# The order of the causal row maxima in a decoder layer's attention: query tiles 2, 3, 0, 1, two heads at a time

## The chip, the core and the metric

One core of one Trainium2 chip runs the whole kernel. The metric is the device time in microseconds (us) of one execution. The engines are TensorE (PE, with its weight loads as PEld), VectorE (DVE), ScalarE (ACT), GpSimd (POOL) and SyncE (SP, which issues most of the DMAs).

## The reference

A decoder layer on x of 8 batches x 512 tokens x 256 features, 16 attention heads of 16 features each:

```
x = x + selfattention(layernorm(x))          # rotary positions, no mask
x = x + (causal selfattention + crossattention with ctx)(layernorm(x)) @ Wp
x = x + moe(x)                               # 16 experts, top 1, capacity 256

att = einsum(q, k) * scale
att = where(tril(ones(T, T)), att, -inf)     # the causal part
y   = einsum(softmax(att), v)
```

So each batch has three attentions: A (without mask), B (causal) and C (with the context). The softmax takes the maximum of each query's row of scores off before the exponential; in B the row of a query ends at its own position.

## The kernel before, in words

**Bodies and slots.** The work is a chain of bodies, numbered -2 to 24 (`plan`, line 257). Bodies 0 to 7 do the A attention of the eight batches; from 8 to 23 a B body (even) and a C body (odd) alternate, one batch for each pair. Bodies 10 to 21 are a hardware loop of six rounds. In bodies 11, 13, ..., 21 (and 23, 24) a batch is also routed to its experts. The experts themselves run at the end, after body 24. Each body has 32 slots. In each slot, every engine's program goes through the same list: it does its share of the maxima, of the exponents, of the product with V, and of the jobs that stand at this slot in a table written by hand (`SLOTS_OF`, line 61; the causal bodies use the entry `BB`, the C bodies `CC`, body 7 `AB`).

**Maxima.** A body has 64 units: 8 pairs of heads x 4 query tiles of 128 x 2 heads of a pair. A slot does two units, the two heads of one pair at one query tile, and it runs 12 slots ahead (`LEAD`, `s_unit` line 446): a body's first 12 slots of maxima run in slots 20 to 31 of the body before, and slots 0 to 19 of the body itself do the rest. `pair_of` (line 452) gives unit u its pair of heads, u // 8, and its query tile, u % 8 // 2. In `maxima` (line 747) TensorE makes the scores of 128 queries against the keys, n columns (line 764): 512 in A and C, and (query tile + 1) x 128 in B, where four masking products (lines 772 and 776) follow. VectorE reduces each half to the negated maximum of its rows (line 1193), into a column of `negmax`. The scores stand in a ring of three buffers, two for each slot: before a slot's scores TensorE waits until the first half of the slot before has been reduced (`max_done`, line 759).

**Hand-over.** Sixteen units make a group of four heads. Two slots after its last unit (slots 5, 13, 21 and 29) TensorE transposes the group's maxima (line 867), ScalarE and VectorE write them as two half-precision rows (lines 1070 and 1296), and SyncE sends these by DMA (line 598) into the stack of queries, so that the product of line 795 takes the maximum off by itself. The exponents' products of a group's first slot (0, 8, 16, 24) wait for that DMA (line 789).

**Exponents.** In slot t TensorE makes the transposed scores of key tile t % 8 // 2 for two heads (line 795; in B 512, 512, 384, 384, 256, 256, 128 and 128 columns over eight slots, in A and C 512 always), and ScalarE their exponentials (line 1029). The product with V (line 741) follows three and four slots later; after each group ScalarE copies it out (line 1021).

**Other work of VectorE around the change.** In a causal body the layer norm of the batch two bodies ahead has its steps in slots 2, 5, 6 and 7 (`layernorm`, line 1137: statistics, small operations, GpSimd's power at line 1427, then the normalizing at line 1165); slot 8 transposes its result (line 831). In slot 7 follows the reciprocal of the softmax sums of the body before (line 1200), which goes to memory and back by DMA, to two products on GpSimd (lines 1473 and 1477) and to ScalarE's cast in slot 16 (line 1001). In the routing C bodies (from 11 on) VectorE makes the one-hot choice in slot 26 (lines 1340 to 1346), TensorE counts with it in slot 27 (line 888), and VectorE works out the places in slot 28 (lines 1350 to 1367). On VectorE the reduces stand first in each slot, then the reciprocal and the norm, then the hand-over, then the routing.

Of the kernel before, what the change touches and what calls it, by code (L numbers as in the profile page):

```python
# [34 lines left out]
P = 128  # L35
NB, T, D, DC = 8, 512, 256, 128
H, HD = 16, 16
TT = T // P
# [267 lines left out]
def need(eng, sem, value):  # L306

    if not isinstance(value, int) or value > 0:
        eng.wait_ge(sem, value)


def build(nc, a):
    blocks, total = plan()
    ctx = ExitStack()
    with ctx:
# [130 lines left out]
        def s_unit(b, t, j):  # L446

            u = 2 * (t + LEAD) + j
            later = u >= S_UNITS
            return later, u % S_UNITS, 2 * t + j if b.kind else 2 * t + j - 2 * (SLOTS - LEAD)  # L450

        def pair_of(u):

            return u // 8, u % 8 // 2

        def has_s(b, later):
            return b.nxt if later else b.kind
# [11 lines left out]
        def stack_of(parity, q_or_k):  # L469
            return stack[:, parity, q_or_k, :].rearrange("p (h t) -> p h t", h=PAIRS)  # L470
# [218 lines left out]
        def _(pe):  # L689
# [24 lines left out]
            for b in stretches(pe, blocks):  # L714
# [11 lines left out]
                for t in range(SLOTS):  # L726
# [20 lines left out]
                    def maxima():  # L747
                        later, u, k = s_unit(b, t, 0)
                        kind = has_s(b, later)
                        if not kind:  # L750
                            return
                        par = np_ if later else b.parity
                        hp, qt = pair_of(u)
                        if later and u == 0:
                            if b.n in (-1, 0):
                                pe.wait_ge(stack_set, 16 * 4)
                            pe.wait_ge(s["stack_in"], b.at("stack_in", 16 * len(LOADS)))

                        need(pe, s["max_done"], b.at("max_done", k - 1))
                        n = (qt + 1) * P if kind == "B" else T  # L760
                        banks = S_BANKS[u // 2]
                        for hh in range(2):
                            rows = slice(PART * hh, PART * hh + STACK)
                            mm = nc.tensor.matmul(psS[:, banks[hh], 0:n], stack_of(par, 0)[rows, hp, qt * P:(qt + 1) * P],  # L764
                                                  stack_of(par, 1)[rows, hp, 0:n], start=True, stop=kind != "B",
                                                  skip_group_check=kind == "B")
                            if kind != "B":
                                mm.then_inc(s["scores_q"], 1)
                        if kind == "B":
                            for hh in range(2):  # L770
                                rows = slice(PART * hh, PART * (hh + 1))
                                nc.tensor.matmul(psS[:, banks[hh], n - P:n], unit_a[rows, :], mask_q[rows, :], start=False,  # L772
                                                 stop=False, skip_group_check=True)
                            for hh in range(2):
                                rows = slice(PART * hh, PART * (hh + 1))
                                mm = nc.tensor.matmul(psS[:, banks[hh], n - PART:n], unit_b[rows, :], mask_q[rows, 0:PART],
                                                      start=False, stop=True, skip_group_check=True)
                                mm.then_inc(s["scores_q"], 1)


                    def exponents():
# [18 lines left out]
                        if b.kind == "B":  # L800
# [4 lines left out]
                            for hh in range(2):  # L805
# [3 lines left out]
                                mm.then_inc(s["scores_k"], 1)  # L809

                    maxima()
                    exponents()
                    if t in b.warm_job:
# [305 lines left out]
        def _(dve):  # L1119
# [50 lines left out]
            for b in stretches(dve, blocks):  # L1170
# [3 lines left out]
                for t in range(SLOTS):  # L1174
# [6 lines left out]
                    for j in range(2):  # L1181
                        later, u, k = s_unit(b, t, j)
                        kind = has_s(b, later)
                        if not kind:
                            continue
                        g = u // (S_UNITS // NG)
                        at = TT * (2 * j + u % 16 // 8) + u % 8 // 2
                        n = (u % 8 // 2 + 1) * P if kind == "B" else T
                        if u % (S_UNITS // NG) == 0:

                            need(dve, s["negmax_rows"], b.at("negmax_rows", t // 8 if b.kind else 0))
                        dve.wait_ge(s["scores_q"], b.at("scores_q", k + 1))
                        nc.vector.tensor_reduce(negmax[:, g % 2, at:at + 1], psS[:, S_BANKS[u // 2][j], 0:n], AX_X, ALU.max,  # L1193
                                                negate=True).then_inc(s["max_done"], 1)
# [407 lines left out]
```

## Time and profile before

| | |
|---|---|
| time of the runs shown | 1627.76, 1622.08, 1626.52 us; median 1626.52 |
| span of the profiled execution | 1626.3 us (its own time is not listed apart) |
| busy share of the span | PE 89%, PEld 40%, DVE 74%, ACT 65%, POOL 40% |
| reduces of line 1193 | 1536, 869.4 us busy |
| bodies | body 8 begins at 521.6 us, body 23 at 1337.9 us |

A row of the timeline has the start and the length of a group of like instructions, its engine, line, operation and tiles; in brackets, how long the engine had been idle before it, and what released it. A row of the windows has, for one stretch, the busy time of each engine and the number of its instructions, then TensorE's mean granted clock as a share of full speed, and the DMA engines' share and GB/s.

### The profile page before, as it was taken

To read this page: it belongs to the slowest core of one execution; us is meant where nothing else is said; L and a number is where in the kernel's file an instruction comes from. 1 tells how busy PE (TensorE), PEld (TensorE's weight loads), DVE (VectorE), ACT (ScalarE), POOL (GpSimd) and SP (SyncE) were. 2 spreads that over 40 slices of the span, in tenths; PEclk is the share of its full clock that TensorE was granted. 3 is DMA by queue.
4 is the path that set the end of the run, shared out by engine and by line. 5 is a ranking of instruction groups with operands and counts; after the bars stand their busy time and mean duration, and the time that the engine had idled before them with its cause. 6 is when DMAs were issued, how large, how long until landed. Compare 5 with 4: busy or idle time off the path is not lost.

```text
span 1626.3 us, 37857 instructions
## 1 busy us (share of the span) xinstructions
PE 1443.6 (89%) x14610; PEld 647.8 (40%) x14610; DVE 1204.3 (74%) x2434; ACT 1062.0 (65%) x2139; POOL 650.5 (40%) x535
## 2 busy tenths in 40 slices
PE   3799999999999898898998989989989978779997
PEld 1222322333333433334334244333343432359997
DVE  6788878888876776776877877768778677537774
ACT  2377777778777676676676676766766656425662
POOL 2544565466422422236145333352352211225554
PEclk8699999999999999999999999999999999889999
DMA  6435344444323433323323322332333211157771
GB/s 179 115 119 141 105 112 115 120 115 112 92 60 95 110 88 101 90 83 104 82 83 88 104 80 69 96 98 71 85 100 97 60 45 39 48 189 262 251 259 62
DMA packets 119479, 175.82 MB, mean 108 GB/s; under 512 B 26273, under 2 KB 85895, under 8 KB 114696
## 3 DMA queue, kind: packets, MB, share of 16 engines
q1 hardware_dynamic: 111376, 158.50, 34.4%
q0 software_dynamic: 5888, 14.24, 2.7%
q8 instruction: 108, 1.77, 0.5%
q10 hardware_dynamic: 2048, 0.83, 0.2%
q14 instruction: 59, 0.48, 0.1%
HBM read 102.33 MB, written 51.18 MB: 94 GB/s over the span
## 4 chain that ended last, share of the span: by engine, by line
PE 54%; DVE 17%; DMA 9%; ACT 6%; issue 6%; POOL 5%; SPq 2%; POOLq 0%; DVEq 0%; ACTq 0%
PE psO L741 13%; PE psM L466 9%; PE psS L764 9%; DVE negmax L1193 9%; PE psK L466 6%; PE psK L795 6%; PE psS L466 4%; ACT probs L1029 4%; DMA recipB<-recip_scratch 3%; PE psK L693 2%; DVE xn L1165 2%; DMA shared<-shared 1%; DVE stats L1141 1%; DMA stack<-mrows 1%; PE psM L831 1%
## 5 line engine op out<-in xcount | busy, mean ns | idle before, releaser
L1193 DVE TENSOR_REDUCE negmax<-psS 128x1 f32<-128x512 f32 (+3 forms) x1536 | 869.4, 615 | 273.6 <-PE psS L764 136.4
L1029 ACT ACTIVATE probs<-psK 128x512 f32<-128x512 f32 (+3 forms) x1536 | 753.7, 544 | 325.3 <-PE psK L795 198.4
L741 PE MATMUL psO<-probs,V 128*32 128x256 f32 (+1 forms) x5632 | 446.1, 389 | 23.8 <-ACT U L1021 17.8
L764 PE MATMUL psS<-stack 48*128 48x512 f16 (+3 forms) x1536 | 284.5, 367 | 57.2 <-DVE negmax L1193 53.7
L795 PE MATMUL psK<-stack 50*128 50x512 f16 (+3 forms) x1536 | 278.5, 359 | 26.1 <-DMA stack<-mrows 14.7
L764 PEld LDWEIGHTS psS<-stack 48*128 48x128 f16 x1536 | 74.2, 93 | 373.2 <-DVE negmax L1193 290.7
L741 PEld LDWEIGHTS psO<-probs,V 128*32 128x32 f32 x5632 | 113.5, 109 | 210.9 <-issue 122.8
L1427 POOL TENSOR_TENSOR rstd<-lnt,minus_half 128x4 f32<-128x4 f32 x24 | 24.7, 1028 | 193.1 <-DVE lnt L1157 193.1
L795 PEld LDWEIGHTS psK<-stack 50*128 50x128 f16 x1536 | 76.5, 95 | 57.4 <-ACT probs L1029 23.6
L1553 POOL DMA_INDIRECT out_dram<-stack,put_to x32 | 76.8, 2399 | 17.8 <-issue 9.1
L1441 POOL CAST shared<-shared 128x512 f16<-128x512 f32 x8 | 4.9, 612 | 191.2 <-ACT shared L1051 191.2
L466 PE MATMUL psM<-xT,wx 128*128 128x512 f16 x288 | 73.3, 382 | 3.8 <-DVE mrows L1296 2.5
L1443 POOL TENSOR_TENSOR parts<-shared,parts 128x512 f16<-128x512 f32 x64 | 74.1, 1158 | 5.1
L1441 POOL CAST parts<-shared 128x512 f16<-128x512 f32 x64 | 39.5, 618 | 76.2 <-ACT shared L1063 76.2
L693 PE MATMUL psK<-wo 128*128 128x512 f16 x224 | 66.4, 390 | 0.4
L1021 ACT COPY U<-psO 128x512 f32<-128x512 f32 x96 | 56.9, 593 | 10.6 <-PE psO L741 9.9
L1521 POOL TENSOR_TENSOR shared<-rs,gate_scale 128x4 f32<-128x4 f32 x8 | 1.7, 206 | 154.5 <-DVE scatter_to L1365 154.5
L772 PE MATMUL psS<-halves 64*128 64x128 bf16 x512 | 57.9, 223 | 0.0
L1473 POOL TENSOR_TENSOR recipB<-packed,recipB 128x1024 f32<-128x1024 f32 x15 | 35.3, 2356 | 54.8 <-DMA recipB<-recip_scratch 54.8
L1063 ACT ACTIVATE shared<-psM,bias_qk 128x512 f32<-128x512 f32 x64 | 44.1, 690 | 18.9 <-PE psM L466 18.9
L807 PE MATMUL psK<-halves 64*128 64x128 bf16 x512 | 55.9, 214 | 0.0
L831 PE MATMUL psM<-consts,xn 128*128 128x128 f32 x184 | 31.6, 297 | 25.2 <-DVE xn L1165 21.4
(192 smaller groups left out, 2063.1 us busy)
## 6 DMA issues: line engine op xcount, KB each, us to landing
spare<-in_L_ffn_w_dram SPq DMA_DIRECT2D x32, 1024.0 KB, 6.3
parts_scratch<-parts SPq DMA_DIRECT2D x192, 128.0 KB
stack<-parts_scratch SPq DMA_DIRECT2D x96, 256.0 KB, 4.0
stack<-parts_scratch SPq DMA_DIRECT2D x96, 128.0 KB, 4.2
packed<-U SPq DMA_DIRECT2D x192, 64.0 KB
recipB<-recip_scratch SPq DMA_DIRECT2D x48, 256.0 KB
shared<-shared SPq DMA_DIRECT2D x48, 128.0 KB, 2.1
probs<-back_scratch POOLq DMA_DIRECT2D x16, 258.0 KB, 3.1
```

Of the source, the lines that this page charges most:

```text
L466: mm = nc.tensor.matmul(out, left(x, k), right(y, k), start=(k, x, y) == steps[0], stop=(k, x, y) == steps[-1])
L693: nc.tensor.matmul(out, wo1[:, 0, 0, 0:P], wo1[:, 0, :, :], start=True, stop=True, skip_group_check=True)
L741: mm = nc.tensor.matmul(psO[32 * i:32 * i + 32, q0:q1], v_of(par)[:, kt, 2 * g + i % 2 + PAIRS * (i // 2), :], probs[:, (unit + i % 2) % P ...
L764: mm = nc.tensor.matmul(psS[:, banks[hh], 0:n], stack_of(par, 0)[rows, hp, qt * P:(qt + 1) * P], stack_of(par, 1)[rows, hp, 0:n], start=Tr ...
L772: nc.tensor.matmul(psS[:, banks[hh], n - P:n], unit_a[rows, :], mask_q[rows, :], start=False, stop=False, skip_group_check=True)
L795: mm = nc.tensor.matmul(psK[:, banks[hh], q0:T], stack_of(b.parity, 1)[rows, hp, kt * P:(kt + 1) * P], stack_of(b.parity, 0)[rows, hp, q0: ...
L807: mm = nc.tensor.matmul(psK[:, banks[hh], q0:q0 + P], unit_b[rows, :], mask_k[rows, :], start=False, stop=True, skip_group_check=True)
L1021: nc.scalar.copy(U[:, g % 2, :], psO[:, :]).then_inc(s["av_out"], 1)
L1029: nc.scalar.activation(probs[:, t % P_RING, i, q0:T], psK[:, S_BANKS[t][i], q0:T], ACT.Exp, scale=SM_SCALE / (1 if b.kind == "A" else WSCA ...
L1193: nc.vector.tensor_reduce(negmax[:, g % 2, at:at + 1], psS[:, S_BANKS[u // 2][j], 0:n], AX_X, ALU.max, negate=True).then_inc(s["max_done"], 1)
L1443: nc.gpsimd.tensor_tensor(lo, src, hi, ALU.subtract).then_inc(s[lo_done], 1)
L1553: nc.gpsimd.indirect_dma_start(out=out_rows_dram, out_offset=bass.IndirectOffsetOnAxis(ap=put_to[:, c, st:st + 1], axis=0), in_=eo_sb[c][: ...
```

## The change

In a causal body's group of eight slots, the query tiles come in the order 2, 2, 3, 3, 0, 0, 1, 1, the two pairs of heads of the group in turn, instead of 0, 1, 2, 3 for one pair and then for the other. A function `tile_of` gives pair and tile for both engines; A and C bodies keep their order. With the lead of 12 slots, slot t % 8 = 0 of a causal body then has tile 0 (128 columns) beside the exponents' 512, slot 2 has tile 1 beside 384, slot 4 has tile 2 beside 256, and slot 6 has tile 3 beside 128.

```
--- before.py
+++ after.py
@@ -449,8 +449,11 @@
             later = u >= S_UNITS
             return later, u % S_UNITS, 2 * t + j if b.kind else 2 * t + j - 2 * (SLOTS - LEAD)
 
-        def pair_of(u):
-
+        def tile_of(kind, u):
+
+            if kind == "B":
+                v = u // 2
+                return 2 * (v // 8) + v % 2, (v % 8 // 2 + 2) % TT
             return u // 8, u % 8 // 2
 
         def has_s(b, later):
@@ -750,7 +753,7 @@
                         if not kind:
                             return
                         par = np_ if later else b.parity
-                        hp, qt = pair_of(u)
+                        hp, qt = tile_of(kind, u)
                         if later and u == 0:
                             if b.n in (-1, 0):
                                 pe.wait_ge(stack_set, 16 * 4)
@@ -1184,8 +1187,9 @@
                         if not kind:
                             continue
                         g = u // (S_UNITS // NG)
-                        at = TT * (2 * j + u % 16 // 8) + u % 8 // 2
-                        n = (u % 8 // 2 + 1) * P if kind == "B" else T
+                        hp, qt = tile_of(kind, u)
+                        at = TT * (2 * j + hp % 2) + qt
+                        n = (qt + 1) * P if kind == "B" else T
                         if u % (S_UNITS // NG) == 0:
 
                             need(dve, s["negmax_rows"], b.at("negmax_rows", t // 8 if b.kind else 0))
```

## Rows read from the trace of the kernel before

**Rows 1.** The page, part 1: busy us, share of the span, instructions of each engine.

```profile
PE 1443.6 (89%) x14610; PEld 647.8 (40%) x14610; DVE 1204.3 (74%) x2434; ACT 1062.0 (65%) x2139; POOL 650.5 (40%) x535
```

**Rows 2.** Windows, body 10: stretch; length, busy us of PE, PEld, DVE, ACT, POOL; PEclk, DMA.

```profile
629.00:638.60 9.60, 7.39 (x117) 3.61 (x113) 8.66 (x28) 4.72 (x14) 1.63 (x2) 1.00 0.35 89
638.60:646.20 7.60, 7.56 (x121) 3.90 (x120) 5.25 (x13) 6.18 (x16) 5.23 (x5) 1.00 0.71 160
```

**Rows 3.** Timeline, body 10, slots 4 to 8: start, length, engine, line, [idle before <- releaser].

```profile
630.26 0.23 PE L764 MATMUL psS<-stack 48*128 48x128 f16 x2
...
630.41 0.27 PE L795 MATMUL psK<-stack 50*128 50x256 f16 x2
...
630.72 0.48 DVE L1193 TENSOR_REDUCE negmax<-psS 128x1 f32<-128x128 f32 x2
...
631.06 0.28 PE L764 MATMUL psS<-stack 48*128 48x256 f16 x2
...
631.47 0.76 DVE L1193 TENSOR_REDUCE negmax<-psS 128x1 f32<-128x256 f32 x2 [0.27 <-PE psS L776]
...
633.94 1.00 DVE L1193 TENSOR_REDUCE negmax<-psS 128x1 f32<-128x384 f32 x2
...
634.53 0.39 PE L764 MATMUL psS<-stack 48*128 48x512 f16 x2 [1.04 <-DVE negmax L1193]
...
634.84 0.22 PE L795 MATMUL psK<-stack 50*128 50x128 f16 x2
...
634.96 0.73 DVE L1165 TENSOR_SCALAR xn<-X,lnt,rstd 128x256 f32<-128x256 f32 x2
...
635.61 1.28 DVE L1193 TENSOR_REDUCE negmax<-psS 128x1 f32<-128x512 f32 x2
...
636.81 0.54 DVE L1200 RECIPROCAL recip<-sums 128x64 f32<-128x64 f32 x1
...
638.05 0.52 PE L831 MATMUL psM<-consts,xn 128*128 128x128 f32 x3 [1.08 <-DVE xn L1165]
```

**Rows 4.** Timeline, body 10, slots 16 and 17.

```profile
651.61 1.04 ACT L1001 CAST attn<-recipB 128x1024 f16<-128x1024 f32 x1 [3.27 <-POOL recipB L1477]
...
653.21 0.39 PE L795 MATMUL psK<-stack 50*128 50x512 f16 x2 [1.26 <-ACT probs L1029]
```

**Rows 5.** Timeline, body 11, slots 26 to the next body's 0; then body 21's end.

```profile
724.84 0.34 PE L764 MATMUL psS<-stack 48*128 48x384 f16 x2
...
725.37 1.02 DVE L1193 TENSOR_REDUCE negmax<-psS 128x1 f32<-128x384 f32 x2 [0.36 <-PE psS L776]
...
727.67 0.17 PE L888 MATMUL psM<-onehot,halves 128*128 128x16 bf16 x1 [0.70 <-DVE onehot L1346]
...
728.67 0.23 PE L764 MATMUL psS<-stack 48*128 48x128 f16 x2
...
729.09 0.49 DVE L1193 TENSOR_REDUCE negmax<-psS 128x1 f32<-128x128 f32 x2 [0.37 <-PE psS L776]
...
731.50 0.75 DVE L1193 TENSOR_REDUCE negmax<-psS 128x1 f32<-128x256 f32 x2
...
731.97 0.34 PE L764 MATMUL psS<-stack 48*128 48x384 f16 x2 [0.85 <-DVE negmax L1193]
...
732.16 0.27 DVE L1296 SCALAR_TENSOR_TENSOR mrows<-psM,mrows 16x128 f16<-16x128 f32 x1
...
734.77 0.39 PE L795 MATMUL psK<-stack 50*128 50x512 f16 x2
...
1283.42 0.27 DVE L1296 SCALAR_TENSOR_TENSOR mrows<-psM,mrows 16x128 f16<-16x128 f32 x1
...
1286.02 0.39 PE L795 MATMUL psK<-stack 50*128 50x512 f16 x2
```

**Rows 6.** Windows, slot 17's exponents to slot 20's, bodies 10 and 12.

```profile
653.21:657.95 4.74, 3.70 (x56) 1.68 (x58) 2.07 (x4) 4.03 (x9) 3.75 (x4) 1.00 0.25 68
763.67:769.67 6.00, 5.00 (x57) 1.91 (x59) 2.31 (x4) 4.11 (x9) 4.01 (x4) 0.74 0.30 86
```

More of the change, by code:

```diff
@@ L450, in s_unit, with tile_of @@
             return later, u % S_UNITS, 2 * t + j if b.kind else 2 * t + j - 2 * (SLOTS - LEAD)
-        def pair_of(u):
+        def tile_of(kind, u):
+            if kind == "B":
+                v = u // 2
+                return 2 * (v // 8) + v % 2, (v % 8 // 2 + 2) % TT
             return u // 8, u % 8 // 2
@@ L752, in maxima @@
                         par = np_ if later else b.parity
-                        hp, qt = pair_of(u)
+                        hp, qt = tile_of(kind, u)
                         if later and u == 0:
@@ L1186, in _ @@
                         g = u // (S_UNITS // NG)
-                        at = TT * (2 * j + u % 16 // 8) + u % 8 // 2
-                        n = (u % 8 // 2 + 1) * P if kind == "B" else T
+                        hp, qt = tile_of(kind, u)
+                        at = TT * (2 * j + hp % 2) + qt
+                        n = (qt + 1) * P if kind == "B" else T
                         if u % (S_UNITS // NG) == 0:
```

## The prediction

> **What bounds the kernel now.** I read the busy shares first. TensorE is busy for 89% of the span and VectorE for 74% [rows 1], but these are averages over stages, so I then went to the stretches in which this change moves anything. They are two: the main stretch (slots 0 to 19 of a causal body), and the lead stretch (slots 20 to 31 of the body before it, where the causal body's first twelve slots of maxima run). Windows over body 10 show two regimes inside the main stretch [rows 2]. In slots 9 to 14 TensorE works 7.56 of 7.60 us and VectorE 5.25: TensorE is the bound. In slots 3 to 8 VectorE works 8.66 of 9.60 us and TensorE only 7.39: VectorE is the bound, because the layer norm of a later batch (slots 5 to 7), the row maxima's hand-over (slot 5) and the reciprocal (slot 7) stand in its queue beside the reduces.
>
> The timeline of slots 4 to 8 shows the chain [rows 3]. The slot 5 reduces end at 632.23; the norm's statistics and the hand-over follow; the slot 6 reduces can start only at 633.94; TensorE waits 1.04 us for the first of them, and another 1.08 us, at 638.05, for the normalized rows that slot 8 transposes. The reciprocal at 636.81 starts a longer chain: out to memory and back, two products on GpSimd, the cast on ScalarE at 651.61, and TensorE's wait of 1.26 us in slot 17 [rows 4].
>
> The lead stretch of a causal body that is preceded by a routing body (11, 13, 15, 17, 19, 21) has a VectorE chain too [rows 5]. TensorE's count waits 0.70 us for the one-hot made behind the slot 26 reduces; the eleven small routing operations stand between the slot 28 and the slot 29 reduces, so that TensorE waits 0.85 us in slot 30; then comes the hand-over (ends 732.43), its DMA, and the next body's first exponents at 734.77, 2.34 us later. The last such body has the same 2.33 us (1283.69 to 1286.02): this hand-over sets when the causal body starts.
>
> **The change, part by part.** No instruction is added or removed, and no wait. What moves are widths. Per head, slots 0 to 3 of a causal body go from 128, 256, 384, 512 columns to 128, 128, 256, 256, and slots 4 to 7 from 128, 256, 384, 512 to 384, 384, 512, 512; so on every eight slots. In the lead stretch, slots 20 to 23 become 384, 384, 512, 512, slots 24 to 27 become 128, 128, 256, 256, and slots 28 to 31 again 384, 384, 512, 512. There the exponents are 512 wide throughout, so the slots are not even after the change: 640 holds only inside the causal body.
>
> Prices: a pair of reduces takes 0.48 us at 128 columns, 0.76 at 256, 1.00 at 384, 1.28 at 512 [rows 3]. On TensorE the two heads run side by side, and 384 columns more move the next operation from 0.15 to 0.31 us behind [rows 3], 0.053 us for 128 columns.
>
> *TensorE alone:* the main stretch loses 512 columns and the lead stretch gains 512, 0.21 us each way. Where TensorE already runs without a gap, an order gives it nothing. So the gain that evener slots might bring must come out of VectorE's waits, and these get longer.
>
> *Main stretch with the norm (bodies 8, 10, ..., 20: seven).* Slot 4's scores start 0.21 us earlier, at 630.05. From a slot's scores to its reduce it takes 0.46 us at 128 columns [rows 3] and 0.53 at 384 [rows 5]; I take 0.50, since the longer value may hold a wait of its own. The 384-wide pair starts at 630.55. Slot 5's scores need its first half: 0.59 us, as from 633.94 to 634.53 [rows 3], so they start at 631.14, the reduces at 631.64, and they end at 632.64 instead of 632.23: 0.41 later. The norm's statistics, the hand-over and the start of the slot 6 reduces move with it; these are now 512 wide, 0.28 more, so the first normalizing operation moves by 0.69. Slot 7 is 512 wide before and after: 0.69 stays, for the reciprocal and for the transposes at 638.05. From slot 9 on TensorE regains 0.21 us by slot 12 and loses it and a little more at slot 13, where 384 columns must be reduced in the time of a slot as short as slot 4 (0.80 us, 630.26 to 631.06 [rows 3]). The reciprocal's chain carries its 0.69 to slot 17 whatever TensorE does between. Slot 19 is then 256 columns shorter: 0.11 back. **0.58 us a body, 4.1 us in all.** The ends: nothing, if the wait in slots 16 and 17 is not for this chain but for transfers that keep their time; 0.9, if slot 13's lateness comes through as well.
>
> *Lead stretch with routing (six).* TensorE reaches slot 26 some 0.11 us later (it has 384 columns more by then, part of which its wait for the logits hides). Slot 26's reduces have 256 columns instead of 384: ready 0.12 us sooner after their scores, and 0.26 shorter. The one-hot and the count come 0.27 us earlier, which is a gain, and slot 28's scores start at 728.40. But they have 384 columns: reduces at 728.93, ending 1.02 later at 729.95 instead of 729.58. The eleven operations then stand 0.37 later, the slot 29 reduces have 384 columns instead of 256, and the hand-over comes 0.37 + 0.27 = **0.64 us later; six times, 3.8 us.** The ends: 0.1 less and more, for the same 0.46 or 0.53. What is lost here cannot be hidden in slots 30 and 31, which are heavier too.
>
> *The other two lead stretches (in bodies 7 and 9)* have no such chain: 0.2 us each for the columns, 0.4. *Body 22's main stretch* has no norm; I put 0.1 for it. All other edits (the column of the stored maxima, the widths' formula) cost nothing: they are worked out when the program is built; the orders of SyncE's and GpSimd's queues, their DMAs included, stay as they are, and only what releases them is late.
>
> Sum: 4.1 + 3.8 + 0.4 + 0.1 = 8.4 us on a span of 1626.3, 1634.7. What lies around the span is not shown; the median of the runs is 0.2 above it, so I forecast **1634.9 us**, 0.5% slower. What a measurement of this kernel can tell from no change is about 0.5%, 8.1 us: the bound is at 1634.7, in the middle of my own forecast.
>
> **A rule against the change.** In slots 3 to 8 TensorE pauses twice for over a microsecond, and the granted clock stays at 1.00, the 2.4 GHz level [rows 2]; my sum keeps it there. The Trainium skill (TensorE: Matmul & The Clock Gate, "HAM oscillation — how this bites in real kernels") warns that a TensorE that pauses between bursts is put back to half its clock. By that rule the longer pauses would cost more than the sum says; by the trace so far they do not.
>
> **The rivals.**
> *The delay is swallowed (faster than forecast, no measurable change).* The main stretch ends in waits for transfers and for ScalarE [rows 4]. If those waits have a cause of their own in most bodies, the 4.1 us go, and 3.8 + 0.4 are left: 1630.7. For it: the waits in slots 15 to 17 differ from body to body. Against it: the chain they wait for begins with the reciprocal, which is itself moved. 0.14.
> *The reduces' waits go away (faster).* TensorE waits 1.04 us in slot 7 [rows 3] and 0.85 us in slot 30 [rows 5] for a reduce. If the lighter slots 0 to 3 and 24 to 27 let VectorE run ahead, so that both waits went, 7 x 1.04 + 6 x 0.85 = 12.4 us would: 1614. It decides in slot 4: VectorE would have to begin its reduces there over 0.6 us earlier, and TensorE's scores come only 0.21 earlier. The lighter slots cannot be saved up, since three buffers hold one and a half slots of scores. 0.05.
> *The longer pauses cost clock (slower).* From slot 17's exponents to slot 20's, body 12 ran at a mean clock of 0.74, partly at 1.2 GHz, and took 6.00 us; body 10, at 1.00 (2.4 GHz), took 4.74 [rows 6]. If each of the seven main stretches lost 1.26 us so, 8.8 us would come on top: 1643.7. For it: the pause before slot 7 grows from 1.0 to about 1.4 us. Against it: the clock at 1.00 through the pauses of today. 0.10. The rule named above from the Trainium skill (TensorE: Matmul & The Clock Gate) would do this.
> *The order does nothing,* since the widths sum to the same and all waits are hidden: 1626.5. Against it are the two waits for a reduce. 0.04.
>
> **How the numbers follow.** My forecast has 0.67; the uncertainty of its terms (0 to 0.9 for the main stretch, 0.1 either way for the lead stretch) and the spread of the runs shown (1622.1 to 1627.8) put a little over half of that, 0.38, above 1634.7 and 0.29 below. Slower by over 0.5%: 0.38 + 0.10 = 0.48. Within 0.5%: 0.29 + 0.14 + 0.04 = 0.47. Faster: 0.05. The range from 1629 to 1642 leaves out the faster rival, the order without effect, and about half of the lost clock.
>
> **What would show it.** Right: in body 10's slot 6 the reduces start about 0.4 us later after slot 4's scores than now, TensorE's pause before slot 7 grows, and the transposes of slot 8 come 0.7 us later after slot 0; in the routed lead stretches the count comes earlier against slot 23 and the hand-over later, by 0.6 us; the 2.3 us from hand-over to first exponents stay. Wrong: a main stretch from slot 0 to slot 20 that is no longer than now, a pause before slot 7 that shrinks, a clock that falls in slots 6 to 8, or a hand-over in slot 29 that is not late.

## The result and the profile after

The changed kernel takes a median of **1634.90 us** over 20 runs (1624.08 to 1649.73); the kernel before, run beside it, 1626.78 over 20 (1615.87 to 1637.06). The ratio is **1.0050, with a 95% interval of 1.0028 to 1.0073**: half a per cent slower, as forecast to the tenth of a microsecond. The profiled execution took 1635.37 us over a span of 1633.6, so 1.8 us lie around the span, which my sum did not have.

The page's part 1 of the kernel after, beside [rows 1]:

```profile
PE 1437.3 (88%) x14610; PEld 643.7 (39%) x14610; DVE 1204.7 (74%) x2434; ACT 1061.5 (65%) x2139; POOL 649.9 (40%) x535
```

Nothing is added: the instruction counts are the same, and VectorE works 1204.7 us in place of 1204.3. The loss is waiting, and the groups of TensorE by line (busy us, mean ns, idle time before, and what ended it) show whose. The scores' row first before, then after:

```profile
L764 PE MATMUL psS<-stack 48*128 48x512 f16 (+3 forms) x1536 | 284.5, 367 | 57.2 <-DVE negmax L1193 53.7
```

```profile
L767 PE MATMUL psS<-stack 48*128 48x512 f16 (+3 forms) x1536 | 284.6, 367 | 67.3 <-DVE negmax L1197 61.6 <-DMA stack<-parts_scratch 2.5 <-issue 0.2
```

TensorE waits 7.9 us longer for reduces (61.6 against 53.7). That is close to the whole loss, but it is not a balance: over the whole span TensorE's idle time grew by 13.6 us and its busy time fell by 6.3, at mean granted clocks of 0.963 before and 0.967 after. (All line numbers rise by 3 or 4 with the change.)

**The main stretch.** Windows of body 10 of the kernel after, for the same two pieces as [rows 2]:

```profile
633.73:644.00 10.27, 7.49 (x117) 3.62 (x113) 8.93 (x28) 4.78 (x14) 1.63 (x2) 1.00 0.34 83
644.00:651.82 7.82, 7.58 (x121) 3.87 (x120) 5.07 (x13) 6.14 (x16) 5.53 (x6) 1.00 0.65 159
```

Slots 3 to 8 take 10.27 us instead of 9.60 and slots 9 to 14 7.82 instead of 7.60, with the clock at 1.00 in both. The timeline of slots 4 to 8, kernel after, answers to [rows 3]. Its times are counted from body 10's first exponents, the first line here (628.985 us, unrounded), against the one line of the kernel before (624.14):

```profile
628.99 0.39 PE L798 MATMUL psK<-stack 50*128 50x512 f16 x2
...
635.38 2.09 DVE L1197 TENSOR_REDUCE negmax<-psS 128x1 f32<-128x384 f32 x4 [0.49 <-PE psS L779]
...
639.19 1.27 DVE L1197 TENSOR_REDUCE negmax<-psS 128x1 f32<-128x512 f32 x2
639.91 0.39 PE L767 MATMUL psS<-stack 48*128 48x512 f16 x2 [1.43 <-DVE negmax L1197]
640.38 0.71 DVE L1168 TENSOR_SCALAR xn<-X,lnt,rstd 128x256 f32<-128x256 f32 x2
642.23 0.53 DVE L1204 RECIPROCAL recip<-sums 128x64 f32<-128x64 f32 x1
643.46 0.63 PE L834 MATMUL psM<-consts,xn 128*128 128x128 f32 x4 [1.08 <-DVE xn L1168]
```

```profile
624.14 0.39 PE L795 MATMUL psK<-stack 50*128 50x512 f16 x2 [0.23 <-ACT probs L1029]
```

From the first exponents: the slot 5 reduces end after 8.49 us (8.09 before), the slot 6 reduces begin after 10.21 (9.80), the normalizing after 11.40 (10.82), the reciprocal after 13.25 (12.67), the transposes after 14.48 (13.91). TensorE's pause before slot 7 grows from 1.04 to 1.43 us, the one before slot 8 stays at 1.08. Up to slot 9 the median of the seven bodies rises from 14.72 to 15.19 us, from there to slot 16's scores from 9.30 to 9.56.

**The end of the main stretch**, body 10, slots 16 and 17, beside [rows 4]:

```profile
655.40 0.39 PE L798 MATMUL psK<-stack 50*128 50x512 f16 x2 [0.58 <-DMA stack<-mrows]
...
656.34 1.04 ACT L1004 CAST attn<-recipB 128x1024 f16<-128x1024 f32 x1 [2.37 <-POOL recipB L1481]
```

The cast follows the reciprocal's end after 13.6 us here, 14.3 before: the transfers in between jitter by more than the 0.57 us at issue (from the reciprocal's end to the product on GpSimd, 6.8 to 9.5 us over the bodies before, 7.5 to 10.7 after).

**The lead stretch with routing.** The timeline of the kernel after, body 13 from slot 26, beside [rows 5]:

```profile
841.94 0.28 PE L767 MATMUL psS<-stack 48*128 48x256 f16 x2
...
844.45 0.17 PE L891 MATMUL psM<-onehot,halves 128*128 128x16 bf16 x1 [0.49 <-DVE onehot L1350]
...
849.52 0.39 PE L767 MATMUL psS<-stack 48*128 48x512 f16 x2 [1.28 <-DVE negmax L1197]
849.85 0.27 DVE L1300 SCALAR_TENSOR_TENSOR mrows<-psM,mrows 16x128 f16<-16x128 f32 x1
850.08 1.08 POOL L1535 DMA_INDIRECT rows_scratch<-xn,scatter_to  x1 [0.87 <-issue]
850.14 1.10 SPq L601 DMA_DIRECT2D stack<-mrows  x2
...
852.74 0.39 PE L798 MATMUL psK<-stack 50*128 50x512 f16 x2 [0.39 <-issue]
```

The count comes 2.51 us after slot 26's scores (2.83 before): the gain I summed. Slot 30 waits 1.28 us (0.85). The hand-over ends 8.18 us after slot 26's scores (7.59 in [rows 5]). The next body's first exponents then follow after 2.62 us, not 2.34: that was not in my sum. From slot 26's scores to the first exponents the median of the six bodies is 10.80 us (9.94 before).

**The clock.** From slot 17's exponents to slot 20's, kernel after, body 10 and body 18, the one causal body of the loop in which the clock fell in this stretch, for the same stretch as [rows 6]:

```profile
657.93:662.46 4.53, 3.48 (x56) 1.71 (x58) 1.62 (x5) 3.93 (x9) 3.54 (x4) 1.00 0.24 65
1105.64:1111.64 6.00, 5.19 (x56) 2.03 (x58) 1.51 (x4) 4.11 (x9) 4.00 (x4) 0.60 0.29 87
```

One body of six at a low clock here, as before. It is not the only place: from body 7's first exponents to body 23's the granted clock falls to its lower level (0.5 of full speed, 1.2 GHz) eight times in the profile before and nine times in the one after, most often in slots 14 to 23 of the C bodies. One of the nine has no like before the change: in body 19 the clock fell in slot 30, right behind TensorE's pause of 1.28 us for a reduce. The rows of the windows from slot 30's scores to the next body's first exponents, kernel after, body 19 and then body 13, which has the same pause:

```profile
1184.99:1189.04 4.05, 4.05 (x38) 1.23 (x40) 3.12 (x6) 2.03 (x4) 2.89 (x3) 0.58 0.26 84
849.52:852.74 3.22, 2.83 (x38) 1.05 (x39) 3.22 (x8) 2.17 (x4) 2.06 (x3) 1.00 0.20 61
```

At a mean clock of 0.58 body 19 takes 4.05 us there, and body 13, at 1.00, 3.22.

**Over everything**, from body 7's first exponents to body 23's, the profile after is 8.2 us longer (877.4 against 869.2). The main stretches with the norm, up to slot 20's scores, give 4.33 of it, the routed leads from slot 26 on 5.78; the rest (-1.9) is not traced to the change. Outside these bodies, where the program is the same, the two profiles differ by +4.6 (bodies 0 to 6) and -5.4 us (from body 23), which is how far one profile alone can be trusted.

### The profile page after: what moved, and what is told of

Read it like the earlier page. It is cut to its first block, busy times and chain, and to the rows that moved or that the text cites. A ratio compares the mean times of both kernels' runs of the same rounds, so it can differ in the third digit from the quotient of the medians.

```text
span 1633.6 us, 37857 instructions
## 1 busy us (share of the span) xinstructions
PE 1437.3 (88%) x14610; PEld 643.7 (39%) x14610; DVE 1204.7 (74%) x2434; ACT 1061.5 (65%) x2139; POOL 649.9 (40%) x535
## 4 chain that ended last, share of the span: by engine, by line
PE 52%; DVE 19%; DMA 9%; issue 7%; ACT 6%; POOL 5%; SPq 2%; POOLq 0%; DVEq 0%; ACTq 0%
PE psO L744 13%; DVE negmax L1197 10%; PE psS L767 9%; PE psM L469 9%; PE psK L469 6%; PE psK L798 6%; ACT probs L1032 4%; PE psS L469 4%; DMA recipB<-recip_scratch 4%; PE psK L696 2%; DVE xn L1168 2%; POOL recipB L1477 1%; DVE stats L1144 1%; DMA shared<-shared 1%; ACT U L1024 1%
## 5 line engine op out<-in xcount | busy, mean ns | idle before, releaser
L767 PE MATMUL psS<-stack 48*128 48x512 f16 (+3 forms) x1536 | 284.6, 367 | 67.3 <-DVE negmax L1197 61.6
L1447 POOL TENSOR_TENSOR parts<-shared,parts 128x512 f16<-128x512 f32 x64 | 74.1, 1157 | 5.1
L516 ACT ACTIVATE V<-spare 128x1024 f16<-128x1024 f32 x32 | 31.9, 1048 | 32.2 <-PE psK L469 32.2
```

Source lines behind the costliest of these rows:

```text
L1447: nc.gpsimd.tensor_tensor(lo, src, hi, ALU.subtract).then_inc(s[lo_done], 1)
```

## The experiments

The theory: the loss is VectorE's queue; wide reduces now stand in the slots where VectorE has other work (slots 5 to 7 and 28). The rivals: the transfers behind the reciprocal set the end of the main stretch; slots of 640 columns help as such; the longer pauses cost clock. The table has medians over the seven main stretches with norm and the six routed leads (us; up to slot 20, where single bodies scatter by several us, the mean), what TensorE waits in the whole kernel for reduces, normalized rows and the one-hot (us, from the rows by line), and the ratio to before with its interval.

| kernel | first exponents to slot 9's | from there to slot 16's scores | first exponents to slot 20's (mean) | slot 26's scores to first exponents | TensorE's waits | ratio |
|---|---|---|---|---|---|---|
| before | 14.72 | 9.30 | 32.99 | 9.94 | 82.6 | |
| after | 15.19 | 9.56 | 33.62 | 10.80 | 89.1 | 1.0050 (1.0028 to 1.0073) |
| slots 4–19 alone | 15.44 | 9.56 | 33.60 | 9.95 | 87.0 | 1.0034 (0.9998 to 1.0069) |
| slots 20–31, 0–3 alone | 14.48 | 9.30 | 33.79 | 10.80 | 84.4 | 1.0051 (1.0017 to 1.0084) |
| slots 20–27 alone | 14.72 | 9.30 | 33.42 | 9.61 | 79.9 | 1.0030 (0.9991 to 1.0069) |
| the same again | 14.80 | 9.30 | 33.83 | 9.62 | 83.2 | 0.9972 (0.9933 to 1.0011) |
| slots 28–31, 0–3 alone | 14.49 | 9.30 | 33.01 | 11.12 | 83.9 | 1.0024 (0.9977 to 1.0070) |
| mirror | 14.03 | 9.18 | 34.19 | 10.00 | 75.8 | 0.9952 (0.9917 to 0.9987) |
| the same again | 14.03 | 9.18 | 33.30 | 10.08 | 74.1 | 0.9968 (0.9931 to 1.0006) |
| mirror, slots 4–19 alone | 13.91 | 9.18 | 33.34 | 9.93 | 76.9 | 0.9963 (0.9921 to 1.0005) |
| mix | 14.02 | 9.18 | 32.15 | 9.32 | 69.6 | 0.9973 (0.9935 to 1.0012) |
| the same again | 14.03 | 9.18 | 32.75 | 9.33 | 71.2 | 0.9937 (0.9901 to 0.9974) |
| norm early | 13.89 | 9.88 | 35.22 | 11.18 | 81.9 | 1.0069 (1.0036 to 1.0101) |
| route late | 15.38 | 9.56 | 33.22 | 10.47 | 90.7 | 1.0049 (1.0009 to 1.0090) |

Each kernel's stretches and waits come from one profiled execution. Those of the mirror (1646.48 us) and of norm early (1659.69) were the longest of their twelve runs; the mirror's stretches up to slot 16 came again in its second profile. The diffs are against the kernel after.

**Half of the change: slots 4 to 19 alone** (the other groups in the old order).

```
-                return 2 * (v // 8) + v % 2, (v % 8 // 2 + 2) % TT
+                if v // 8 > 1:
+                    return 2 * (v // 8) + v % 2, (v % 8 // 2 + 2) % TT
```

> The new order in groups 2 and 3 only, that is in slots 4 to 19 of the causal bodies; the lead stretch and slots 0 to 3 as in the kernel before. Theory (VectorE's queue): slots 4 to 7 are as heavy as after the change, without the lighter slots 0 to 3 ahead of them, so from a causal body's first exponents to those of slot 9 it takes 15.3 to 15.5 us in bodies 8 to 18 (14.7 before, 15.2 after), and from the scores of slot 26 of a routing body to the next body's first exponents 9.9 us as before (10.5 to 10.8 after); total about 5 us over before. Rival (transfers): both stretches within their scatter of the kernel before, the total too. Rival (even slots help): slots 4 to 19, now even, are shorter than before.

Both stretches came as expected, 15.44 and 9.56 us, and the lead stayed at 9.95. The ratio, 1.0034, is 5.5 us, but its interval reaches just below 1. In body 14 the granted clock fell at the end of slot 7, behind a pause of 1.43 us, and the stretch to slot 9 took 16.00 us.

**The other half: slots 20 to 31 and 0 to 3 alone** (`if v // 8 < 2:` in the same place).

> The new order in groups 0 and 1 only, that is in the lead stretch and in slots 0 to 3 of the causal bodies. Theory (VectorE's queue): from slot 26's scores of a routing body to the next body's first exponents 10.5 to 10.8 us as after the change (9.9 before); in the causal bodies slots 0 to 3 are 0.2 us shorter and slots 4 to 8 as before, so first exponents to slot 9's in 14.4 to 14.6 us; total about 2.5 us over before. Rival (transfers): no difference to before that can be told in either stretch.

The stretches came as expected; the total lies more above before than their sum, though the interval reaches down to 1.0017. So, as far as these stretches go, the two halves of the prediction are separate, and each is where it was put: the old order of slots 4 to 19 keeps the first stretch at 14.5, the old order of slots 20 to 31 keeps the lead at 9.95.

**The mirror.** The light tiles in the second half of each eight slots, where VectorE has its other work.

```
-                return 2 * (v // 8) + v % 2, (v % 8 // 2 + 2) % TT
+                return 2 * (v // 8) + v % 2, v % 8 // 2
```

> The same pairs of slots, but tiles 0, 0, 1, 1, 2, 2, 3, 3: the slots of a causal body now have 896 or 384 columns, the most uneven sum, and slots 4 to 7, where the norm and the reciprocal stand, have reduces of 128 and 256 columns. Theory (VectorE's queue): first exponents to slot 9's in 14.1 to 14.3 us (0.5 less than before, 1.0 less than after); slot 26's scores to the next body's first exponents 9.9 to 10.1 us; total 3 to 4 us under before, so about 12 under after. Rival (even slots help TensorE): slower than both, by 0.3 us a body or more. Rival (transfers): as before.

Faster than before in this comparison (the interval of its repeat, below, reaches 1.0006). Slots of 896 and 384 columns beat the even ones, whose interval lies wholly above, so evenness is not what counts. The stretch to slot 9, 14.03 us, is a little shorter than the 14.1 to 14.3 expected: up to there it counts that slots 4 to 7 are light. In the mirror the pause before slot 7 is 0.63 us and that before slot 8 is 0.69.

**The layer norm earlier.** The change, with the norm's steps in slots 1, 2, 4 and 5.

```
-           "ln": (2, 5, 6, 7), "load": (1, 2, 3, 6, 7, 8, 9, 10), "split": (10, 11, 14, 17, 20, 23), "store": (16, 18, 21, 25),
+           "ln": (1, 2, 4, 5), "load": (1, 2, 3, 6, 7, 8, 9, 10), "split": (10, 11, 14, 17, 20, 23), "store": (16, 18, 21, 25),
```

> The change as it is, with the layer norm of causal bodies in slots 1, 2, 4 and 5 instead of 2, 5, 6 and 7. Theory (VectorE's queue): TensorE's pauses before slot 7 (1.43 us) and in slot 8 (1.08) go, first exponents to slot 9's in 12.6 to 13.0 us (15.2 after); the reciprocal is 2 us earlier, and if its transfers keep their durations the main stretch is 1.5 to 2 us shorter to slot 20: total 10 to 13 us under after, 2 to 5 under before. Rival (transfers set the end of the main stretch): first exponents to slot 9's shrink, but slots 15 to 18 grow by as much, and the total is that of after.

A miss: 1.0069. The first stretch did shrink in four bodies of seven, but only to 13.6 to 13.9 us, not to the 12.6 to 13.0 expected, and in body 12 it took 16.73. The timeline of body 12, norm early:

```profile
754.02 0.97 POOL L1535 DMA_INDIRECT back_scratch<-shared,scatter_to  x1 [0.30 <-issue]
755.01 1.07 POOL L1431 TENSOR_TENSOR rstd<-lnt,minus_half 128x4 f32<-128x4 f32 x1
...
756.11 0.73 DVE L1168 TENSOR_SCALAR xn<-X,lnt,rstd 128x256 f32<-128x256 f32 x2 [1.49 <-POOL rstd L1431]
...
757.37 0.39 PE L767 MATMUL psS<-stack 48*128 48x512 f16 x2 [1.76 <-DVE negmax L1197]
```

GpSimd's queue is full of the scatter's eight issues until 755.0, the norm's power stands behind them, VectorE waits 1.49 us for it with the reduces behind, and TensorE 1.76. Some 2 us later the granted clock falls as well: from 759.5 to 762.8 us it is 0.50, the 1.2 GHz level. I had moved a step past a queue and not counted what stands in that queue. That this is what made the median slower is not shown: the lines are of one body of a long execution, and the rest of the loss (9.88 us to slot 16, the leads at 11.18) I did not follow up.

**The mix.** Slots 20 to 27 as in the change, all others mirrored: light tiles in slots 24 to 31 and 4 to 7, where the count, the hand-over, the norm and the reciprocal are.

```
-                return 2 * (v // 8) + v % 2, (v % 8 // 2 + 2) % TT
+                return 2 * (v // 8) + v % 2, (v % 8 // 2 + 2 * (v < 8)) % TT
```

> Slots 20 to 27 in the order of the change (tiles 2, 2, 3, 3, 0, 0, 1, 1), all other groups in the order 0, 0, 1, 1, 2, 2, 3, 3: the light tiles stand in slots 24 to 31 and 4 to 7, where VectorE has the count, the hand-over and the normalizing. VectorE's queue as the bound: in the six leads with routing, slot 26's scores to the next body's first exponents take 9.0 to 9.4 us (9.94 before, 10.8 after), the hand-over's end to the first exponents 2.33; first exponents to slot 9's take 13.9 to 14.2 us (14.7 before, 15.19 after), from there to slot 16's scores 9.18 (9.30, 9.56). Sum: 6 x 0.7 and 7 x 0.75 = 9.5 us under before, ratio 0.994. The reciprocal's transfers as the bound of the main stretch: only the leads' 4 us are left, ratio 0.9975. Even slots as such help: slower than before, since no slot has 640 columns outside of slots 20 to 27.

All three stretches came as expected. The ratio did not: 0.9973 is what the transfers as the bound would give (0.9975) and not the sum's 0.994, though the interval holds both; it was tried again below. The timeline of the mix, body 10's slots 7 and 8 and body 13's end:

```profile
640.97 0.28 PE L767 MATMUL psS<-stack 48*128 48x256 f16 x2 [0.64 <-DVE negmax L1197]
...
644.09 0.63 PE L834 MATMUL psM<-consts,xn 128*128 128x128 f32 x4 [0.69 <-DVE xn L1168]
...
845.49 0.28 PE L767 MATMUL psS<-stack 48*128 48x256 f16 x2 [0.72 <-DVE negmax L1197]
845.55 0.27 DVE L1300 SCALAR_TENSOR_TENSOR mrows<-psM,mrows 16x128 f16<-16x128 f32 x1
...
845.84 1.10 SPq L601 DMA_DIRECT2D stack<-mrows  x2
...
846.31 1.09 POOL L1535 DMA_INDIRECT rows_scratch<-xn,scatter_to  x1 [0.87 <-issue]
...
848.13 0.39 PE L798 MATMUL psK<-stack 50*128 50x512 f16 x2
```

The waits of the kernel after stand against these: 1.43, 1.08 and 1.28 us. The hand-over here goes out ahead of the scatter, and the first exponents follow it by 2.31 us.

**Slots 20 to 27 alone** (`if v < 8:`) and **slots 28 to 31 and 0 to 3 alone** (`if v // 8 == 1:`), the rest in the old order. They take the lead's terms apart.

> Only slots 20 to 27 in the new order. VectorE's queue: the count starts earlier, so slot 26's scores to slot 28's take 3.51 us as after (3.83 before), and the rest of the lead is as before (6.1 us to the first exponents, hand-over to first exponents 2.33): 9.6 us in all (9.94 before, 10.8 after); the main stretch as before (14.7 us, 9.30 us). Sum 6 x 0.32 = 1.9 us under before, ratio 0.999. If what the count gains is waited away in slots 28 to 31, 9.94 us and 1.000.

> Only slots 28 to 31 and 0 to 3 in the new order. VectorE's queue: slot 26's scores to slot 28's 3.83 us as before, from there to the first exponents 7.0 to 7.3 us (6.1 before), in all 10.9 to 11.1 us, with the later hand-over 2.6 us ahead of the first exponents (2.33 before) because its second DMA lands behind the scatter; first exponents to slot 9's 14.45 us (14.7 before). Sum 6 x 1.05 - 7 x 0.25 = 4.5 us over before, ratio 1.003. If the hand-over's 0.27 us came from the earlier count and not from the scatter, the hand-over would stay at 2.33 and the lead at 10.6.

Both leads came as expected: 9.61 us with the earlier count alone, 11.12 with the later hand-over alone; neither term was waited away. The kernel with slots 28 to 31 in the new order, body 13's end (its lines are one higher):

```profile
848.82 0.39 PE L768 MATMUL psS<-stack 48*128 48x512 f16 x2 [1.28 <-DVE negmax L1198]
...
849.14 0.27 DVE L1301 SCALAR_TENSOR_TENSOR mrows<-psM,mrows 16x128 f16<-16x128 f32 x1
...
849.37 1.08 POOL L1536 DMA_INDIRECT rows_scratch<-xn,scatter_to  x1 [0.87 <-issue]
849.44 1.10 SPq L602 DMA_DIRECT2D stack<-mrows  x2
...
852.03 0.39 PE L799 MATMUL psK<-stack 50*128 50x512 f16 x2 [0.38 <-issue]
```

The 2.62 us come with the later hand-over and not with the earlier count. The ratio of slots 20 to 27 alone, 1.0030, lay above its sum (0.999); this too was tried again below.

**The mirror in slots 4 to 19 alone.**

```
-                return 2 * (v // 8) + v % 2, (v % 8 // 2 + 2) % TT
+                if v // 8 > 1:
+                    return 2 * (v // 8) + v % 2, v % 8 // 2
```

> Only slots 4 to 19 in the order 0, 0, 1, 1, 2, 2, 3, 3; slots 20 to 31 and 0 to 3 as before. VectorE's queue: first exponents to slot 9's 13.7 to 13.9 us (14.7 before, 15.43 with the new order here), from there to slot 16's scores 9.18, the lead as before (9.94, hand-over 2.33). Sum 7 x 1.05 = 7.4 us under before, ratio 0.9955. The reciprocal's transfers as the bound: the stretches are the same but slots 16 to 19 take 1 us longer each body, and the ratio is 0.9985 to 1.000.

13.91 and 9.18 us as expected. The ratio, 0.9963, lies nearer to the queue's 0.9955 than to the transfers' 0.9985 or more, but its interval holds both. The profile speaks for the transfers: the bodies reach slot 16's scores 0.88 us sooner than before (mean of seven), but from there to slot 20's exponents they take 10.13 us instead of 8.90, and slot 20 comes no sooner than before (33.34 against 32.99).

One profile cannot settle it, since that last piece takes 7.4 to 10.9 us in single bodies of the kernel before. Thirteen profiles together say more (all of the table but norm early, whose norm stands elsewhere; seven bodies each):

| order in slots 4 to 19 | profiles | first exponents to slot 16's scores, mean | from there to slot 20's exponents, mean | first exponents to slot 20's, mean |
|---|---|---|---|---|
| new (after; slots 4–19 alone; route late) | 3 | 25.00 | 8.49 | 33.48 |
| old (before; slots 20–31, 0–3; slots 20–27 twice; slots 28–31, 0–3) | 5 | 24.02 | 9.39 | 33.41 |
| mirrored (mirror twice; mirror, slots 4–19 alone; mix twice) | 5 | 23.21 | 9.93 | 33.15 |

The last two columns have a standard error of some 0.3 us. Of the 1.8 us between the new and the mirrored order at slot 16, 0.3 are left at slot 20. The times speak the other way: the mirror (0.9952 and 0.9968) and this kernel gain some 6 us, with intervals of about 6 us to either side, although their leads gain nothing. So how much of a main stretch's gain or loss arrives stays open; that all of it does is not shown.

**The route's last part one slot later**, to see whether the scatter delays the hand-over.

```
-           "attn": 20, "bias": 2, "route": (6, 9, 13, 15), "chain": (23, 25, 26, 28, 28), "exp": 24,
+           "attn": 20, "bias": 2, "route": (6, 9, 13, 15), "chain": (23, 25, 26, 28, 29), "exp": 24,
```

> The change, with the last part of the route chain (which ends in the scatter's index) on VectorE behind slot 29's maxima in place of slot 28's. If the later hand-over waits behind the scatter's packets because the index now leads it by 1.19 us (0.93 before): the index comes two reductions later and leads by some 0.3 us, the hand-over's end stays where it is and the first exponents follow it by 2.33 us in place of 2.62, so slot 26's scores to the first exponents take 10.5 us (10.8 after, 9.94 before), some 6 x 0.28 = 1.7 us under the kernel after in all. If the 0.27 us have nothing to do with the scatter's place: 2.62 and 10.8 as after. If the later scatter itself holds something up, it shows as a new wait in slots 0 to 6 of the next body, whose first exponents to slot 9's take over 15.2 us.

The lead came out at 10.47 us, the number expected, but for another reason. The timeline of body 13's end, route late:

```profile
840.68 0.28 DVE L1300 SCALAR_TENSOR_TENSOR mrows<-psM,mrows 16x128 f16<-16x128 f32 x1
...
842.27 0.15 DVE L1369 TENSOR_TENSOR scatter_to<-rs 128x4 uint32<-128x4 f32 x1
...
843.15 0.39 PE L767 MATMUL psS<-stack 48*128 48x512 f16 x2 [1.55 <-DVE negmax L1197]
...
844.57 0.38 PE L798 MATMUL psK<-stack 50*128 50x512 f16 x2
```

In slot 29 the hand-over stands ahead of the route on VectorE, which I had overlooked: it now ends at 840.96, before the index, and the first exponents come 3.61 us later. They no longer wait for it. TensorE waits 1.55 us in slot 31 for reduces that stand behind the route instead. Read so, 0.33 of the 0.86 us that the routed lead lost hang on the hand-over being last, and 0.53 (10.47 against 9.94) remain with VectorE's queue; since this run also puts the route behind one more pair of reduces, that split is an argument and not shown. Whether the scatter alone makes the 0.27, this run cannot say. The later scatter itself may hold something up: up to slot 9 three bodies take 15.2 us, three 15.4 and one 16.0.

**Three kernels again**, side by side on one chip: does the new order of slots 20 to 27 have a price that the stretches do not show?

> The same kernel as the mix, beside the mirror and the group-0 kernel on one chip: does the new order of slots 20 to 27 cost something that the stretches do not show? By the stretches it is 4.0 us shorter than the mirror (6 x 0.67), and 9 to 11 us shorter than before: ratio 0.994. If the new order of slots 20 to 27 has a hidden price of some 7 us, as the two ratios so far would have it (1.003 where 0.999 was summed, 0.9973 where 0.994 was), it lies 3 us over the mirror: 0.9975.

> By the stretches 6 us shorter than before: ratio 0.9963, between the mix and the kernel before. With the hidden price it lies under the mix. A look at the profile too: first exponents to slot 9's 14.0, from there to slot 16's scores 9.18, lead 10.0 us.

> Only slots 20 to 27 in the new order. By the stretches 1.9 us shorter than before: ratio 0.999. With a hidden price of 7 us in these slots: 1.003 again.

No: 0.9937, 0.9968 and 0.9972, each within 0.002 of the sum by stretches (0.994, 0.9963, 0.999), with the mix fastest. The same kernels had stood at 0.9973, 0.9952 and 1.0030 the first time; the means of the two are 0.9955, 0.9960 and 1.0001. The mix is faster than the kernel before, its second interval ending at 0.9974 (the first reaches 1.0012), and than the kernel after by about 1%, across two comparisons; that it beats the mirror as well is told by the stretches (0.7 us in each routed lead), not by the times.

## Why the prediction was right

- **The bound.** That VectorE's queue and not TensorE sets slots 3 to 8 and 28 to 30 was the ground of all terms. It held: the same widths in other slots give 13.9 to 15.4 us up to slot 9, and the ratios follow TensorE's waits by and large, from 69.6 us in the mix to 90.7 with the route late (norm early is an exception, and the first ratio of slots 20 to 27 alone).
- **The main stretch, +0.58 a body.** Up to slot 9 the steps are as worked out: the slot 5 reduces 0.41 late by the sum, 0.40 measured; the slot 6 reduces' 0.28 more, 0.27 measured. The normalizing moved by 0.58 instead of 0.69: before the change it started 0.02 us behind the end of the reduces, 0.03 behind the end of GpSimd's power (which starts at 633.91 and takes 1.02 us); after it 0.08 ahead of the end of the reduces, with the power done 0.17 us before. So 0.1 us of slack took part of the delay. The transposes of slot 8 moved by the same 0.57. Slot 13's lateness, which I had counted as swallowed but for the upper end, came through up to slot 16's scores (+0.27). Over the seven bodies 4.33 us up to slot 20's scores, by one profile, where I had 4.1; that agreement is luck. The step "the reciprocal's chain carries its 0.69 to slot 17 whatever TensorE does between" is not borne out: over thirteen profiles the new order is 0.98 us behind the old at slot 16 and 0.07 at slot 20, each mean with a standard error of some 0.3 there. My lower end, nothing, lies as near to the profiles as the 4.1.
- **The routed lead.** The count 0.32 us earlier (0.27 by the sum), the hand-over 0.59 later after slot 26 (0.53: the forecast's 0.64 less the 0.11 by which slot 26 is late). The term that was mis-sized is "the 2.3 us from hand-over to first exponents stay": in bodies 13, 15, 17 and 21 they became 2.6, and in body 19 3.46, of which the 0.84 over 2.62 are the low clock shown above and no DMA. So the leads cost 5.78 us from slot 26 on, where my terms make 6 x 0.53 = 3.2. What made up for it in the total is not worked out by the change: slots 20 to 25 of these leads, which vary between 10.6 and 13.2 us in both kernels, were 3.1 us shorter in sum in this profile, where I had each 0.11 longer.
- **Bodies 7 and 9, and 22.** Nothing in the first two from slot 20 on (0.4 summed; -0.2 measured), and body 22 was 1.0 shorter by its transfers (0.1 summed).
- **The rivals.** The reduces' waits did not go away, they grew by 7.9 us; slots 0 to 3, though lighter, could not be saved up. The order did something. In this profile the clock stayed at 1.00 through the pauses of 1.43 and 1.08 us in slots 7 and 8, in all seven bodies; with slots 4 to 19 alone it fell there in one body of seven. The pause before slot 30, which the rival did not name, was followed by a fall more often: in 7 of the 24 routed leads of the four kernels in which it has grown to some 1.28 us (after; slots 20 to 31 and 0 to 3; slots 28 to 31 and 0 to 3; norm early), and in none of the 30 leads of the five profiles with the old order in slots 28 to 31, where it is 0.86 or less. The seven take 3.3 to 3.5 us from hand-over to first exponents. So the lost clock is out in slots 6 to 8 of this profile but has a part of the truth in the leads, 0.84 us in one of six here; that the pause brings it about is likely by these counts and not tried by itself. The Trainium skill (TensorE: Matmul & The Clock Gate, "HAM oscillation — how this bites in real kernels") warns that TensorE is put back to half its clock when it pauses between bursts. The rows of this profile do not show it for the pauses of slots 7 and 8, and show it behind one of the six before slot 30. The fall in body 18 came behind a longer wait, for ScalarE in slot 17; its stretch is the one of 6.00 us at 0.60 above. The timeline of the kernel after:

```profile
1105.64 0.39 PE L798 MATMUL psK<-stack 50*128 50x512 f16 x2 [2.44 <-ACT probs L1032]
```

  Such a stretch was there before as well [rows 6]. That the delay is swallowed, to which I gave 0.14, is what the thirteen profiles show for most of the main stretch's term; the times leave it open, as said above.
- **The numbers.** The median met the forecast exactly, which the terms do not deserve: it is luck. They missed by +2.6 us in the leads from slot 26 on and by 3.7 the other way in slots 20 to 25, and the main stretch's 4.1 may not arrive in full. The interval of the ratio (1.0028 to 1.0073) is what they can be held to.

## What to carry to other kernels

When a fixed set of pieces of different width is spread over slots, level the engine that is the bound in each slot, with all that stands in its queue there, and not the columns of two kinds of TensorE work: the wide pieces belong where that engine has nothing else. Read from the slot's timeline which engine TensorE waits for; then the order that puts the light pieces under the other jobs (the mix) follows. Then follow the gain to the end of the body: a wait for transfers behind it can take it back, as slots 16 to 20 seem to do here. A step that is moved to an earlier slot joins the queue of every engine it uses, GpSimd's scatter included.

## What was not expected of the hardware

- **Which of two DMAs is issued first seems to matter by 0.27 us.** Within one program, the kernel after, body 11's hand-over is issued ahead of GpSimd's scatter and the first exponents come 2.34 us after its end; in body 13 the scatter's issue is 0.06 us ahead (850.08 and 850.14, above) and they come after 2.62. Body 11's end in the kernel after:

```profile
735.39 0.27 DVE L1300 SCALAR_TENSOR_TENSOR mrows<-psM,mrows 16x128 f16<-16x128 f32 x1
...
735.68 1.10 SPq L601 DMA_DIRECT2D stack<-mrows  x2
735.76 1.22 POOL L1535 DMA_INDIRECT rows_scratch<-xn,scatter_to  x1 [1.01 <-issue]
...
738.00 0.39 PE L798 MATMUL psK<-stack 50*128 50x512 f16 x2
```

  The rows of the mix (hand-over first, 2.31 us, with TensorE not waiting for the DMA at all) and of slots 28 to 31 alone (scatter first, 2.62) agree. So do the other routed leads of all profiles but route late's: with the hand-over first (55 leads) 2.31 to 2.38 us, but for one of 3.27 at the low clock, and with the scatter first (23 leads) 2.54 or more. It is read off, not tried by itself.
- **The same kernel, measured twice, differed by 0.0016 to 0.0058 in its ratio,** each time with intervals of some 0.0037 to either side. The stretches of a profile up to slot 16, which in most bodies of a kernel agree to some 0.1 us, told the kernels apart far sooner; those from slot 16 to 20, which scatter by 3 us and more, do not.
